# Order of the recurrence's exponential, spreading and state products, and attention positions computed four sequences ahead

## The chip, the cores and the metric

The kernel runs on one core of one Trainium2 chip. The metric is the device time of one execution in microseconds. The core's engines work side by side and meet at semaphores: TensorE (PE, and PEld for its weight loads), VectorE (DVE), ScalarE (ACT), GpSimd (POOL), and SyncE (SP), whose queue issues the transfers.

## The reference

The reference is an audio tower of four layers on 64 sequences of 250 frames (246 tokens after the front end), width 128. Two of its parts matter here; both are cut to their core.

The delta-rule attention of layer 2 walks over the batch axis as its time: 64 steps, for each of 246 positions (`bsz`) and 8 heads of size 64, once for `z` and then for the recurrence:

```python
def rec_step(carry, inp):
    R, h = carry
    zt, kt, vt, bt = inp
    qh = jax.nn.softmax(h, axis=-1)
    v_old = jnp.einsum('bhij,bhj->bhi', R, kt)
    R = R + (bt * (vt - v_old))[..., :, None] * kt[..., None, :]
    h = zt + jnp.einsum('bhij,bhj->bhi', R, qh)
    return ((R, h), h)
```

The kernel has the rows `u = bt * (vt - v_old)` from an earlier stage, so a step is h[t] = zz[t] + ri * sum over s up to t of (k[s] . e) u[s], with e the exponential of h[t-1] less its maximum, and ri one over the sum of e.

The relative attention of layer 3, for each of 64 sequences:

```python
matrix_bd = jnp.matmul(q_v, p.transpose(0, 1, 3, 2))
matrix_bd = rel_shift(matrix_bd)[:, :, :, :T] * scale
scores = jnp.matmul(q_u, k.transpose(0, 1, 3, 2)) * scale + matrix_bd
attn = jax.nn.softmax(scores, axis=-1)
out = jnp.matmul(attn, v)
```

## The kernel before

The kernel is a row of stages, each with its own buffers and semaphores; a stage consists of blocks, in which every engine has its own hand-written order, and at the end of a block all engines meet. Two stages are touched.

**Recurrence (`recur_stage`).** `run` is called 8 times, for pairs of heads and halves of the positions. One run holds 123 positions by 2 heads, split in group 0 (62 positions, 124 chains) and group 1 (61, 122 chains), one chain to a partition, and goes through SL = 64 steps t. In a step below HC = 32, each group `a` passes these operations:

- VectorE `dots(a, t)`: the product of the keys so far with `e` (L2945, 64 x n elements with n = t+1), its sum (L2950), and the weights `w` (L2954), which release TensorE;
- TensorE `turn(a, t)`: transposes `w` into `wT` (L2866);
- ScalarE `spread(a, t)`: writes `wT` into the block-diagonal `W` (L2816);
- TensorE `recent(a, t)`: the products of `W` with the values, into `acc` (L2894); one block of values up to 16 steps, two above;
- VectorE `finish(a, t)`: `acc` times the reciprocal plus `H` (L2964), and its maximum (L2965);
- ScalarE `exped(a, t)`: the exponential and its sum (L2828), on which the next `dots` of the group waits.

For 12 <= t < 32 (`inside`) VectorE puts `finish(1, t-1)` between the product and the sum of group 0. From step HC on, the 32 first steps act through a state: `make_state(n)` on TensorE (L2908) computes the state of 8 positions from keys and values (`Ks`, `Us`), `keep_state(n)` on ScalarE copies it (L2834). There are NR = 16 such parts, one in each step from RT0 = 14 to 29, of which TensorE does each between `recent(0, t)` and `turn(1, t)`, and ScalarE each after `spread(0, t)`. From step 32 on, `state(a, t)` multiplies with them, and ScalarE already has the exponential of group 0 ahead of group 1's spreading. The first state product of step 32 waits for `turn_exp`, which stands behind `recent(1, 31)`.

**Relative attention (`relative_stage`).** G = 16 sequences make one pass. For a new sequence j of a pass ("positions"): A projects queries, B multiplies them with the position matrix in 8 parts, ScalarE's `kept` copies these to `BD` (L3839, two buffers in turn; it waits until the store of two sequences before has landed), and SP stores them to `scr` in DRAM (L3622). The skewed read back from `scr` into `sc` (L3607, three buffers in turn) gives the shifted matrix. For a current sequence: projections (C, V; the values are written at L3767), scores S, softmax, T transposes, P, O. PSUM is a ring of four buffers through which all these products pass in the order that `order` lists.

`step_of(new, cur)` writes a pass: positions for the 16 sequences of block `new`, and everything else for the 16 of block `cur`. Before, a prologue makes positions for block 0 alone, three loop passes do block i with the positions of block i+1, and a last pass does block 3 without any. The read of current sequence j+2 is issued on SP when the scores of j-1 have been turned.

Of the kernel before, what the change touches and what calls it, by code (L numbers as in the profile page):

```python
# [12 lines left out]
B = 64  # L13
# [3 lines left out]
T = TIN - CTX + 1  # L17
# [2197 lines left out]
SL = B  # L2215
# [469 lines left out]
def recur_stage(nc, c, kr, ur, zz, hs):  # L2685


    SC, HC = 16, 32
# [6 lines left out]
    with Stage(nc, "recur") as st:  # L2695
# [72 lines left out]
        def run(i, half, following):  # L2768
            with st.step() as block:
# [40 lines left out]
                @block.scalar  # L2810
                def _(act):
                    def spread(a, t):
                        n = t % HC + 1
                        act.wait_ge(s_tr[a], t + 1)
                        r, b = (8 * n, 1) if n <= SC else (128, 2)
                        nc.scalar.activation(W[a][0:r, 0:b].rearrange("p b (g x) -> p b g x", x=40)[:, :, :, 0:8],  # L2816
                                             wT[a][0:r, 0:b].rearrange("p b (g x) -> p b g x", x=8), ACT.Copy).then_inc(s_dg[a], 1)

                    def spread_exp(a, t):
                        tg = GROUPS[a][1]  # L2820
                        act.wait_ge(s_et[a], t - HC + 1)
                        nc.scalar.activation(E[a][:, 0:34 * TG].rearrange("p (m x) -> p m x", x=34)[:, 0:tg, 0:2],
                                             eT[a][:, 0:2 * tg].rearrange("p (m h) -> p m h", h=2), ACT.Copy).then_inc(s_eg[a], 1)

                    def exped(a, t):
                        cp = 2 * GROUPS[a][1]
                        act.wait_ge(s_mx[a], t + 1)
                        nc.scalar.activation(e[a][0:cp], Hh[a][0:cp, t, :], ACT.Exp, bias=mx[a][0:cp, 0:1],  # L2828
                                             accum_out=rs[a][0:cp, 0:1]).then_inc(s_ex[a], 1)

                    def keep_state(n):
                        a, m0, nm = positions(n)
                        act.wait_ge(s_rm, n + 1)
                        nc.scalar.activation(R[a][:, m0:m0 + nm, :], Rp[n % 2][:, 0:nm, :], ACT.Copy).then_inc(s_rc, 1)  # L2834

                    for t in range(SL):
                        if t > HC:
                            exped(1, t - 1)
                            spread(0, t)
                            spread_exp(1, t)  # L2840
                        else:
                            if inside(t):
                                exped(1, t - 1)
                            spread(0, t)
                            if t and not inside(t):
                                exped(1, t - 1)
                            if t == HC:
                                spread_exp(1, t)
                        if RT0 <= t < RT0 + NR:
                            keep_state(t - RT0)  # L2850
                        if t + 1 < SL and t >= HC:
                            exped(0, t)
                        spread(1, t)
                        if t + 1 < SL and t < HC:
                            exped(0, t)
                        if HC <= t + 1 < SL:
                            spread_exp(0, t + 1)

                @block.tensor
                def _(pe):  # L2860
# [50 lines left out]
                    for t in range(SL):  # L2911
                        if t and t % SC == 0:
                            pe.wait_ge(s_in[t // SC], 16 * 24)
                        if t < HC:
                            for a in range(2):
                                turn(a, t)
                                recent(a, t)
                                if a == 0 and RT0 <= t < RT0 + NR:
                                    make_state(t - RT0)
                            if t == HC - 1:  # L2920
                                turn_exp(0, HC)
                        else:
# [563 lines left out]
def relative_stage(nc, c, xnT, pT, Wq, bq, Wk, bk, Wv, bv, Wo, bo, pu, pv_, scr, h, h_out):  # L3486


    SCALE = HD ** -0.5
    G = 16  # L3490
    NR = 3
    QH = NH // 2
    SCORES_AT = {0: 0, 2: 1, 5: 2, 7: 3}
    with Stage(nc, "rel") as st:
# [75 lines left out]
                dve.wait_ge(s_g, 1)  # L3570
                own(V.tensor_tensor(brow[:], brow[:], ring[0][0:HT, 0, 0:D], ALU.add))

        xblk = lambda n: xnT[:, bass.ds(n * (G * T), G * T)]
        rows = lambda t, n: t.rearrange("(i n p) d -> i p n d", n=2 * G, p=HT)[n]

        def step_of(new, cur):

            NX = new is not None
            CU = cur is not None
            proj = lambda j: [("A", j)] * NX + [("C", j), ("V", j)] * CU  # L3580
            order = proj(0)
            for j in range(G + 2):
                for q in range(8 if j < G else 0):
                    order += [("S", j, SCORES_AT[q])] if CU and q in SCORES_AT else []
                    order += [("B", j, q)] * NX
                    order += [("O", j - 2)] * (CU and j >= 2 and q == 3)
                if CU and j >= G:
                    order.append(("O", j - 2))
                if j + 1 < G:
                    order += proj(j + 1)  # L3590
                if CU and 1 <= j <= G:
                    order += [("T", j - 1, q) for q in range(4)] + [("P", j - 1)]
# [6 lines left out]
            with st.step() as block:  # L3599
                @block.sync  # L3600
                def _(sp):
# [4 lines left out]
                                n = p.stop - p.start  # L3606
                                sp.dma_start(sc[j % NR][p, f], bass.AP(scr.tensor, o, [[NH * WB - 1, n], [WB, NH], [1, T]])).then_inc(s_bd[j % NR][f], 16)  # L3607

                    if NX:
                        sp.dma_start(xa[:].rearrange("p a t -> p (a t)"), xblk(new)).then_inc(s_xa, 16)  # L3610
                    if CU:
                        sp.dma_start(xc[:].rearrange("p a t -> p (a t)"), xblk(cur)).then_inc(s_xc, 16)
                        for j in range(2):
                            positions(j)
                        for p in PARTS:
                            sp.dma_start(hb[p], rows(h, cur)[p]).then_inc(s_hb, 16)
                    for j in range(G + 2):
                        if NX and j < G:
                            for f in range(2):
                                sp.wait_ge(s_da, act_upto("B", j, 4 * f + 3))  # L3620
                                for p in PARTS:
                                    sp.dma_start(scr[new * (2 * G) + (2 * j + f)][p], BD[j % 2][f][p]).then_inc(s_bw[j % 2], 16)  # L3622
                        if CU and j + 2 < G:
                            if j:
                                sp.wait_ge(s_g, at["T", j - 1, 3] + 1)
                            positions(j + 2)
                        if CU and j >= 2:
                            sp.wait_ge(s_dd, dve_upto("O", j - 2))
                            for p in PARTS:
                                sp.dma_start(rows(h_out, cur)[p, 2 * j - 4:2 * j - 2], hb[p, 2 * j - 4:2 * j - 2]).then_inc(s_out, 16)  # L3630
                    if NX:
                        for k in range(2):
                            sp.wait_ge(s_bw[k], 64 * (G // 2))
                    if CU:
                        sp.wait_ge(s_out, 32 * G)

# [1 line left out]
                def _(pe):  # L3638
# [82 lines left out]
                        ins.then_inc(s_g, 1)  # L3721

                    def project(j):
                        if NX:
                            queries_next(j)
                        if CU:
                            queries_keys(j)
                            values(j)

                    project(0)  # L3730
                    for j in range(G + 2):
                        for q in range(8 if j < G else 0):
                            if CU and q in SCORES_AT:
                                scores(j, SCORES_AT[q])
                            if NX:
                                positions(j, q)
                            if CU and j >= 2 and q == 3:
                                outs(j - 2)
# [10 lines left out]
                def _(dve):  # L3749
# [5 lines left out]
                                                      hp[:].unsqueeze(2).to_broadcast(full), ALU.add, ALU.mult)  # L3755

                    def projected(j):
                        if NX:
                            dve.wait_ge(s_g, at["A", j] + 1)
                            masked(QV, slot("A", j), 3).then_inc(s_dd, 1)  # L3760
                        if CU:
# [59 lines left out]
                def _(act):  # L3821
# [25 lines left out]

                    for j in range(G + 1):
                        for q in range(8):
                            if NX and j < G:  # L3850
                                kept(j, q)
                            if CU and j and q < 4:
                                exped(j - 1, q)
# [1 line left out]
                            for q in range(4):  # L3855
                                turned(j - 1, q)

        step_of(0, None)
        with nc.Fori(0, B // G - 1) as i:
            step_of(i + 1, i)  # L3860
        step_of(None, B // G - 1)


def last_stage(nc, c, Wg, bg, We, be, h, out):
# [306 lines left out]
```

## Time and profile before

| | |
|---|---|
| median of 3 runs | 18497.64 us |
| lowest to highest | 18490.13 to 18520.3 us |
| profiled execution | 18509.24 us |
| its span, first to last instruction | 18507.2 us |
| mean granted TensorE clock | 0.787 of full speed |
| PE busy | 13100.1 us (71%) |
| DVE busy | 10585.8 us (57%) |
| ACT busy | 6518.6 us (35%) |
| recurrence, all 8 runs | about 10212 to 15040 us of the span |
| attention: prologue | first issue at 16300.77 us |
| attention: three loop passes | first issues at 16479.34, 16919.81 and 17359.78 us |
| attention: last pass | first issue at 17796.96 us, next stage at 18207.04 us |

Busy time counts an engine's instructions, not its waits. Times in rows are microseconds from the span's start. A line number is the kernel's, or that of the helper that records the operation: all projections and products of the attention stage show as L3640.

### The profile page before, as it was taken

What the parts mean: (1) busy time and instruction counts of PE and PEld (TensorE: products, weight loads), DVE (VectorE), ACT (ScalarE), POOL (GpSimd) and SP (SyncE); (2) the same over time, 40 slices, a digit from 0 to 9 for tenths busy, and PEclk for the clock granted to TensorE, in tenths of its full rate; (3) what the DMA queues carried; (4) which work ended last, traced back from release to release, by engine and by line L of the source; (5) the groups of instructions that cost most, each with busy time, mean ns of one, the idle gap of its engine ahead of it and who ended that gap; (6) DMA issues with size and microseconds to landing.
All of it is one profiled execution on the core that took longest, in us unless ns stands there. A gap on an engine that the chain in (4) does not pass through costs nothing. (4 is left out here: it accounts for less than half of the span.)

```text
span 18507.2 us, 593329 instructions
## 1 busy us (share of the span) xinstructions
PE 13100.1 (71%) x262069; PEld 10249.8 (55%) x262069; DVE 10585.8 (57%) x24424; ACT 6518.6 (35%) x16019; POOL 2265.2 (12%) x1394
## 2 busy tenths in 40 slices
PE   4607778862847888888888667766677675867777
PEld 3505666651535676766766455555555564735555
DVE  6451457763144555555555676767776745346664
ACT  3101246640214565665665112121211121345541
POOL 0048100003541111111111000000000000000001
PEclk9556578875868999999999667866787697967775
DMA  0313320121331111111111222021211153177752
GB/s 22 106 30 46 69 48 21 33 77 45 65 76 46 24 26 26 26 24 26 26 24 26 47 42 43 19 44 38 45 33 28 38 129 93 39 228 195 195 136 68
DMA packets 1835030, 1095.27 MB, mean 59 GB/s; under 512 B 1109166, under 2 KB 1763409, under 8 KB 1814481
## 3 DMA queue, kind: packets, MB, share of 16 engines
q1 hardware_dynamic: 1605063, 999.32, 22.4%
q0 software_dynamic: 227328, 57.19, 2.1%
q8 instruction: 2092, 34.28, 0.8%
q14 instruction: 547, 4.48, 0.1%
HBM read 569.43 MB, written 484.53 MB: 57 GB/s over the span
## 5 line engine op out<-in xcount | busy, mean ns | idle before, releaser
L2894 PE MATMUL recur_acc<-recur_U,recur_W 8*32 8x64 f32 (+4 forms) x49152 | 1402.4, 270 | 510.3 <-ACT recur_W L2816 428.5
L2894 PEld LDWEIGHTS recur_acc<-recur_U,recur_W 8*32 8x32 f32 (+4 forms) x49152 | 1068.8, 140 | 928.8 <-ACT recur_W L2816 738.6
L2945 DVE TENSOR_TENSOR recur_pr<-recur_K,recur_e 124x64 f32<-124x64 f32 (+60 forms) x1024 | 1282.0, 1252 | 395.9 <-ACT recur_e L2828 395.6
L2881 PE MATMUL recur_acc<-recur_R,recur_E 128*32 128x64 f32 x62976 | 1206.6, 232 | 247.1 <-issue 235.4
L2950 DVE TENSOR_REDUCE recur_dot<-recur_pr 124x1 f32<-124x64 f32 (+60 forms) x1024 | 1281.8, 1252 | 29.8
L2881 PEld LDWEIGHTS recur_acc<-recur_R,recur_E 128*32 128x32 f32 x62976 | 1070.1, 118 | 350.0 <-issue 294.0
L2475 ACT ACTIVATE delta_B0l<-delta_pS 64x256 f32<-64x256 f32 x1968 | 743.4, 378 | 875.4 <-PE delta_pS L2375 857.9
L2816 ACT ACTIVATE recur_W<-recur_wT 128x256 f32<-128x256 f32 (+16 forms) x1024 | 335.1, 327 | 1961.2 <-PE recur_wT L2866 1960.0
L2866 PE MATMUL recur_wT<-const_ident,recur_w 128*128 128x128 f32 (+15 forms) x1536 | 479.5, 375 | 768.1 <-DVE recur_w L2954 760.9
L2475 ACT ACTIVATE delta_B1l<-delta_pS 64x256 f32<-64x256 f32 x1968 | 743.6, 378 | 698.8 <-PE delta_pS L2375 678.2
L2375 PE MATMUL delta_pM<-delta_B1l 64*64 64x128 f32 (+1 forms) x11808 | 737.2, 255 | 140.8 <-ACT delta_B1l L2478 140.3
L2375 PE MATMUL delta_pM<-delta_B0l 64*64 64x128 f32 (+1 forms) x11808 | 720.8, 256 | 66.5 <-ACT delta_B0l L2478 66.4
L2510 POOL TENSOR_TENSOR delta_QK<-delta_QK,delta_mx 128x512 f32<-128x512 f32 x369 | 384.6, 1042 | 3116.3 <-DVE delta_mx L2563 3116.3
L2375 PE MATMUL delta_gp<-delta_W,delta_xc 128*128 128x512 f32 x1230 | 696.0, 650 | 54.8 <-DVE delta_xc L2546 36.1
L2375 PEld LDWEIGHTS delta_pM<-delta_B1l 64*64 64x64 f32 x11808 | 602.6, 134 | 165.0 <-ACT delta_B1l L2478 158.7
L2375 PE MATMUL delta_gp<-delta_KT 64*64 64x64 f32 x11808 | 563.5, 224 | 183.7 <-ACT delta_KT L2497 143.2
L2375 PEld LDWEIGHTS delta_pM<-delta_B0l 64*64 64x64 f32 x11808 | 580.8, 133 | 197.1 <-issue 112.9
L2866 PEld LDWEIGHTS recur_wT<-const_ident,recur_w 128*128 128x128 f32 (+15 forms) x1536 | 168.9, 143 | 931.4 <-DVE recur_w L2954 833.9
L2964 DVE SCALAR_TENSOR_TENSOR recur_H<-recur_acc,recur_ri,recur_H 124x64 f32<-124x64 f32 (+1 forms) x1024 | 284.8, 278 | 676.2 <-PE recur_acc L2894 669.1
L2828 ACT ACTIVATE recur_e<-recur_H,recur_mx 124x64 f32<-124x64 f32 x1008 | 346.8, 344 | 915.6 <-DVE recur_mx L2965 915.3
L2375 PE MATMUL delta_pM<-delta_B 64*64 64x128 f32 x7872 | 548.1, 278 | 136.1 <-issue 87.5
L3188 POOL IOTA choice_ios<- 123x64 f32 x1 | 0.2, 184 | 5245.6 <-POOLq L78 5245.6
(620 smaller groups left out, 34022.7 us busy)
## 6 DMA issues: line engine op xcount, KB each, us to landing
scr<-rel_BD SPq DMA_DIRECT2D x128, 1288.0 KB
rel_sc<-scr SPq DMA_DIRECT2D x128, 861.0 KB
xnT<-ln_xT SPq DMA_DIRECT2D x64, 492.0 KB, 3.0
kr<-delta_QK SPq DMA_DIRECT2D x492, 64.0 KB, 2.4
ur<-delta_Uf SPq DMA_DIRECT2D x492, 64.0 KB, 2.3
zz<-delta_Z SPq DMA_DIRECT2D x492, 64.0 KB, 2.2
recur_K<-kr SPq DMA_DIRECT2D x64, 448.0 KB
recur_H<-zz SPq DMA_DIRECT2D x64, 448.0 KB
```

The lines of the kernel that those rows point to most:

```text
L2375: return nc.tensor.matmul(o, l, r, start=True, stop=True)
L2475: ins = nc.scalar.activation(new[h, :, 0, :], pS[k][HALF[1 - x], 0:4, :], ACT.Copy)
L2510: nc.gpsimd.tensor_tensor(third(j), third(j), mx[:, rows_of(j)].unsqueeze(2).to_broadcast([128, FH, FD]), ALU.subtract).then_inc(s_sh, 1)
L2816: nc.scalar.activation(W[a][0:r, 0:b].rearrange("p b (g x) -> p b g x", x=40)[:, :, :, 0:8], wT[a][0:r, 0:b].rearrange("p b (g x) -> p b g ...
L2828: nc.scalar.activation(e[a][0:cp], Hh[a][0:cp, t, :], ACT.Exp, bias=mx[a][0:cp, 0:1], accum_out=rs[a][0:cp, 0:1]).then_inc(s_ex[a], 1)
L2866: ins = nc.tensor.transpose(wT[a][0:8 * k, b, :], w[a][:, SC * b:SC * b + k, :].rearrange("p s k -> p (s k)"), c.ident[:])
L2881: nc.tensor.matmul(acc[a][32 * q:32 * q + 32, 0:FD], E[a][:, EQ * q + 32 * j:EQ * q + 32 * j + 32], R[a][:, m, :], start=(j == 0), stop=False)
L2894: ins = nc.tensor.matmul(acc[a][32 * q:32 * q + 32, 0:FD], W[a][0:8 * k, b, 160 * q + 32 * j:160 * q + 32 * j + 32], U[a][0:8 * k, 2 * (t ...
L2945: V.tensor_tensor(pr[0:cp, 0:n, :], K[a][0:cp, r0:r0 + n, :], e[a][0:cp, None, :].to_broadcast([cp, n, FD]), ALU.mult).then_inc(s_own[a], 1)
L2950: own[a](V.tensor_reduce(dot[a][0:cp, 0:n], pr[0:cp, 0:n, :], AX.X, ALU.add))
L2964: own[a](V.scalar_tensor_tensor(Hh[a][0:cp, t, :], acc[a][0:cp, 0:FD], ri[a][0:cp, 0:1], Hh[a][0:cp, t, :], ALU.mult, ALU.add))
L3188: nc.gpsimd.iota(ios[:], pattern=[[1, CS]], base=0, channel_multiplier=0, allow_small_or_imprecise_dtypes=True).then_inc(s_po, 1)
```

## The change

In the recurrence, steps 12 to 31: ScalarE takes `exped(0, t)` before `spread(1, t)` in place of after it, as it does from step 32 on. TensorE makes the state part of a step after `recent(1, t)` in place of before `turn(1, t)`. ScalarE keeps it one step later, before `spread(0, t)`.

In the attention stage, `step_of` takes the first new sequence, the current block and the number of sequences ahead. The prologue makes positions of LAG = 4 sequences; loop pass i those of sequences 16i+4 to 16i+19; the last pass those of the last 12. So a stored position matrix can be read in the pass that writes it, and SP gets a wait for its store ahead of the read.

```diff
                             if inside(t):
                                 exped(1, t - 1)
+                            if RT0 < t <= RT0 + NR:
+                                keep_state(t - 1 - RT0)
                             spread(0, t)
...
-                        if RT0 <= t < RT0 + NR:
-                            keep_state(t - RT0)
-                        if t + 1 < SL and t >= HC:
+                        early = t >= HC or inside(t)
+                        if t + 1 < SL and early:
                             exped(0, t)
                         spread(1, t)
-                        if t + 1 < SL and t < HC:
+                        if t + 1 < SL and not early:
                             exped(0, t)
...
                             for a in range(2):
                                 turn(a, t)
                                 recent(a, t)
-                                if a == 0 and RT0 <= t < RT0 + NR:
-                                    make_state(t - RT0)
+                            if RT0 <= t < RT0 + NR:
+                                make_state(t - RT0)
...
+    LAG = 4
...
-        xblk = lambda n: xnT[:, bass.ds(n * (G * T), G * T)]
+        xblk = lambda first, count: xnT[:, bass.ds(first * T, count * T)]
...
-        def step_of(new, cur):
-
-            NX = new is not None
+        def step_of(new, cur, ahead):
+
+            NX = lambda j: j < ahead
...
-                        sp.dma_start(xa[:].rearrange("p a t -> p (a t)"), xblk(new)).then_inc(s_xa, 16)
+                        sp.dma_start(xa[:, 0:ahead, :].rearrange("p a t -> p (a t)"), xblk(new, ahead)).then_inc(s_xa, 16)
...
                         if CU and j + 2 < G:
                             if j:
                                 sp.wait_ge(s_g, at["T", j - 1, 3] + 1)
+                            n = j + 2 - LAG
+                            if n >= 0:
+                                sp.wait_ge(s_bw[n % 2], 64 * (n // 2 + 1))
                             positions(j + 2)
...
-        step_of(0, None)
+        step_of(0, None, LAG)
         with nc.Fori(0, B // G - 1) as i:
-            step_of(i + 1, i)
-        step_of(None, B // G - 1)
+            step_of(i * G + LAG, i, G)
+        step_of(B - G + LAG, B // G - 1, G - LAG)
```

The remaining lines replace the condition `NX` by `NX(j)`, and the block counts by sequence counts.

## Rows read from the trace of the kernel before

**Rows 1.** Windows, steps 12 to 31, then after step 32: busy, count; clock, DMA
```profile
10275.00:10480.00 205.00, 126.11 (x2836) 96.16 (x2835) 162.79 (x240) 38.67 (x137) 0.00 (x0) 0.50 0.08 17
...
10483.00:10513.00 30.00, 24.73 (x1052) 19.98 (x1054) 9.55 (x44) 6.29 (x26) 0.00 (x0) 0.90 0.10 22
```
**Rows 2.** Grouped lines, whole span, then 10275 to 10480: busy, mean ns, idle before
```profile
L2945 DVE TENSOR_TENSOR recur_pr<-recur_K,recur_e 124x64 f32<-124x64 f32 (+60 forms) x1024 | 1282.0, 1252 | 395.9 <-ACT recur_e L2828 395.6
...
L2945 DVE TENSOR_TENSOR recur_pr<-recur_K,recur_e 124x832 f32<-124x832 f32 (+39 forms) x40 | 65.9, 1649 | 35.8 <-ACT recur_e L2828 35.8
```
**Rows 3.** Timeline, steps 21 to 22: start, duration, engine, operation, [idle before, releaser]
```profile
10364.50 1.97 PE L2908 MATMUL recur_Rp<-recur_Us,recur_Ks 32*64 32x64 f32 x32
10364.55 0.34 DVE L2954 TENSOR_TENSOR recur_w<-recur_dot,recur_par 122x176 f32<-122x176 f32 x1
...
10365.18 0.22 DVE L2965 TENSOR_REDUCE recur_mx<-recur_H 124x1 f32<-124x64 f32 x1
...
10366.40 0.69 PE L2866 MATMUL recur_wT<-const_ident,recur_w 128*128 128x128 f32 x2
...
10367.12 0.38 ACT L2816 ACTIVATE recur_W<-recur_wT 128x256 f32<-128x256 f32 x1
...
10367.40 0.34 ACT L2828 ACTIVATE recur_e<-recur_H,recur_mx 124x64 f32<-124x64 f32 x1
...
10367.56 2.09 PE L2894 MATMUL recur_acc<-recur_U,recur_W 128*32 128x64 f32 x64 [0.47 <-ACT recur_W L2816]
10367.64 0.19 ACT L2828 ACTIVATION_READ_ACCUMULATOR recur_e<-recur_H,recur_mx 124x1 f32 x1
...
10367.86 1.69 DVE L2945 TENSOR_TENSOR recur_pr<-recur_K,recur_e 124x1472 f32<-124x1472 f32 x1 [2.46 <-ACT recur_e L2828]
...
10369.72 0.28 DVE L2964 SCALAR_TENSOR_TENSOR recur_H<-recur_acc,recur_ri,recur_H 122x64 f32<-122x64 f32 x1 [0.16 <-PE recur_acc L2894]
...
10371.88 0.35 DVE L2954 TENSOR_TENSOR recur_w<-recur_dot,recur_par 124x184 f32<-124x184 f32 x1
```
**Rows 4.** Timeline of the attention's prologue: its load, first product, fourth and sixteenth copies
```profile
16300.77 0.33 SPq L3610 DMA_DIRECT2D rel_xa<-xnT  x1
...
16307.83 1.19 PE L3640 MATMUL rel_ring<-rel_xa,rel_w 128*128 128x246 f32 x2 [9.42 <-DMA rel_xa<-xnT]
...
16337.58 5.52 ACT L3839 ACTIVATE rel_BD<-rel_ring 123x736 f32<-123x736 f32 x8 [5.08 <-DMA scr<-rel_BD]
...
16459.46 5.52 ACT L3839 ACTIVATE rel_BD<-rel_ring 123x736 f32<-123x736 f32 x8 [3.79 <-DMA scr<-rel_BD]
```
**Rows 5.** Timeline, loop pass, then last pass: first issue, first and thirteenth values
```profile
16479.34 0.38 SPq L3610 DMA_DIRECT2D rel_xa<-xnT  x1
...
16494.55 0.68 DVE L3767 TENSOR_TENSOR rel_Vp<-rel_ring,rel_mk 123x512 f32<-123x512 f32 x1
...
16786.81 0.68 DVE L3767 TENSOR_TENSOR rel_Vp<-rel_ring,rel_mk 123x512 f32<-123x512 f32 x1
...
17796.96 0.37 SPq L3612 DMA_DIRECT2D rel_xc<-xnT  x1
...
17807.23 0.68 DVE L3767 TENSOR_TENSOR rel_Vp<-rel_ring,rel_mk 123x512 f32<-123x512 f32 x1
...
18086.69 0.68 DVE L3767 TENSOR_TENSOR rel_Vp<-rel_ring,rel_mk 123x512 f32<-123x512 f32 x1
```
**Rows 6.** Timeline: one-block products; VectorE's product at steps 17 and 31
```profile
10295.67 1.08 PE L2894 MATMUL recur_acc<-recur_U,recur_W 120*32 120x64 f32 x32 [0.47 <-ACT recur_W L2816]
...
10314.15 1.36 DVE L2945 TENSOR_TENSOR recur_pr<-recur_K,recur_e 124x1152 f32<-124x1152 f32 x1 [2.69 <-ACT recur_e L2828]
...
10468.43 2.29 DVE L2945 TENSOR_TENSOR recur_pr<-recur_K,recur_e 124x2048 f32<-124x2048 f32 x1 [0.97 <-ACT recur_e L2828]
```
**Rows 7.** Timeline of a loop pass: reads of a sequence's positions, that sequence's values
```profile
16611.76 2.12 SPq L3607 DMA_DIRECT2D rel_sc<-scr  x4
...
16633.48 0.68 DVE L3767 TENSOR_TENSOR rel_Vp<-rel_ring,rel_mk 123x512 f32<-123x512 f32 x1
```

More of the change, by code:

```diff
@@ L3571, in _ @@
                 own(V.tensor_tensor(brow[:], brow[:], ring[0][0:HT, 0, 0:D], ALU.add))
-        xblk = lambda n: xnT[:, bass.ds(n * (G * T), G * T)]
+        xblk = lambda first, count: xnT[:, bass.ds(first * T, count * T)]
         rows = lambda t, n: t.rearrange("(i n p) d -> i p n d", n=2 * G, p=HT)[n]
-        def step_of(new, cur):
-            NX = new is not None
+        def step_of(new, cur, ahead):
+            NX = lambda j: j < ahead
             CU = cur is not None
-            proj = lambda j: [("A", j)] * NX + [("C", j), ("V", j)] * CU
+            proj = lambda j: [("A", j)] * NX(j) + [("C", j), ("V", j)] * CU
             order = proj(0)
@@ L3584, in step_of @@
                     order += [("S", j, SCORES_AT[q])] if CU and q in SCORES_AT else []
-                    order += [("B", j, q)] * NX
+                    order += [("B", j, q)] * NX(j)
                     order += [("O", j - 2)] * (CU and j >= 2 and q == 3)
@@ L3607, in positions @@
                                 sp.dma_start(sc[j % NR][p, f], bass.AP(scr.tensor, o, [[NH * WB - 1, n], [WB, NH], [1, T]])).then_inc(s_bd[j % NR][f], 16)
-                    if NX:
-                        sp.dma_start(xa[:].rearrange("p a t -> p (a t)"), xblk(new)).then_inc(s_xa, 16)
+                    if ahead:
+                        sp.dma_start(xa[:, 0:ahead, :].rearrange("p a t -> p (a t)"), xblk(new, ahead)).then_inc(s_xa, 16)
                     if CU:
-                        sp.dma_start(xc[:].rearrange("p a t -> p (a t)"), xblk(cur)).then_inc(s_xc, 16)
+                        sp.dma_start(xc[:].rearrange("p a t -> p (a t)"), xblk(cur * G, G)).then_inc(s_xc, 16)
                         for j in range(2):
@@ L3617, in _ @@
                     for j in range(G + 2):
-                        if NX and j < G:
+                        if NX(j):
                             for f in range(2):
@@ L3621, in _ @@
                                 for p in PARTS:
-                                    sp.dma_start(scr[new * (2 * G) + (2 * j + f)][p], BD[j % 2][f][p]).then_inc(s_bw[j % 2], 16)
+                                    sp.dma_start(scr[new * 2 + (2 * j + f)][p], BD[j % 2][f][p]).then_inc(s_bw[j % 2], 16)
                         if CU and j + 2 < G:
@@ L3630, in _ @@
                                 sp.dma_start(rows(h_out, cur)[p, 2 * j - 4:2 * j - 2], hb[p, 2 * j - 4:2 * j - 2]).then_inc(s_out, 16)
-                    if NX:
+                    if ahead:
                         for k in range(2):
-                            sp.wait_ge(s_bw[k], 64 * (G // 2))
+                            sp.wait_ge(s_bw[k], 64 * (ahead // 2))
                     if CU:
@@ L3723, in project @@
                     def project(j):
-                        if NX:
+                        if NX(j):
                             queries_next(j)
@@ L3734, in _ @@
                                 scores(j, SCORES_AT[q])
-                            if NX:
+                            if NX(j):
                                 positions(j, q)
@@ L3757, in projected @@
                     def projected(j):
-                        if NX:
+                        if NX(j):
                             dve.wait_ge(s_g, at["A", j] + 1)
@@ L3849, in _ @@
                         for q in range(8):
-                            if NX and j < G:
+                            if NX(j):
                                 kept(j, q)
```

## The prediction

> **What bounds the kernel now.** I read first the page of the profile: no engine is full, so the kernel is a row of stages with limits of their own, and only two of them are touched. For the first, the recurrence, I read the granted clock and the grouped lines of a stretch that covers steps 12 to 31 of one run, then the timeline of one step there. For the second, the relative-position attention, I read its timeline at the prologue, at a loop pass and at the last pass.
>
> In steps 12 to 31 of a run, 205 us, VectorE is the engine that everything turns around, and it sits idle 35.8 us in 20 waits for group 0's exponential; the whole span has 395.6 us of that wait, 49.5 for each of the 8 runs, so 35.8 of a run's 49.5 lie here [rows 2]. The timeline of step 21 shows why [rows 3]. Group 1's weights `w` are ready to be turned at 10364.55+0.34 = 10364.89; call this point A. VectorE finishes group 0 and has its maximum at 10365.18+0.22 = A+0.51. The exponential could start then. But TensorE makes state products until 10366.4, only then turns group 1's weights, ScalarE spreads them at 10367.12, and the exponential, queued behind that spreading, starts at 10367.40. VectorE goes on at 10367.86, 2.46 us after its maximum.
>
> In the attention stage, the prologue computes positions for 16 sequences alone. ScalarE needs 5.52 us for each, but waits for the store of two sequences before: its start moves from 16337.58 to 16459.46 in 12 sequences, 10.16 us each, released by the DMA [rows 4]. From its first values to its thirteenth a loop pass takes 24.4 us a sequence, the last pass, which has no positions, 23.3 [rows 5].
>
> **Part 1, the recurrence (steps 12 to 31 of 8 runs).** After the edit the exponential of group 0 follows the maximum at once. Row by row: maximum at A+0.51, exponential 0.04 later (A+0.55; an estimate, ScalarE takes a turn 0.03 after its end at 10367.09), VectorE goes on 0.46 after its start, as 10367.40 to 10367.86 does: A+1.01. So each wait becomes 0.50 us. What is late next is group 1: its spreading now stands behind the exponential and its accumulator read. These end at +0.43 (0.24 from exponential to read, 0.19 the read), A+0.98; from spreading to products is 0.44 (10367.12 to 10367.56), and from products to the finish that waits for them 2.16 (10367.56 to 10369.72): A+3.58 [rows 3]. VectorE is ready for that finish 0.08 before its product of length D ends: A+0.93+D. So a new wait of 2.65-D stands in front of "finish group 1". D is 1.36 us at step 17 and 2.29 at step 31, 0.066 more with each step [rows 6]; the 15 waits sum to 15 x 2.65 less 15 x 1.825, or 12.4 us. Steps 13 to 16 follow one block: the products take 1.08 in place of 2.09 [rows 6] and I put the spreading 0.1 shorter, so the wait is about 1.54-D, with D from 1.10 to 1.29 by the same slope: 1.4 us for the four.
>
> The same formula gives what this wait is today: the products start at 10367.56, 0.30 before VectorE's own product, so it is 1.94-D, or 2.8 us over steps 17 to 25 (at step 22 it is 0.25; the row's 0.16 is counted from the product's nominal end). Sum for one run: before 35.8+2.8 = 38.6; after 0.67 for step 12 (it has the old order ahead of it; 0.67 is what steps 12 to 14 show), 19 x 0.50 = 9.5, 12.4 and 1.4, or 24.0. Gain 14.6. At step 32 the state products queue behind group 1's recent products, which are 0.43 later against A, so 14.2 remain. Times 8: **114 us**. Steps 13 to 16 are where the edit's two sides nearly cancel; steps 17 to 22 gain 1.3 to 1.6 us each.
>
> The state products move behind group 1's. TensorE is free of them at A+0.98+0.44+2.02+1.90 = A+5.34, and next has to turn group 0's weights, which follow the finish by 2.16+0.3 at step 22 (10369.72 to 10371.88, and its own time) and by 0.33 less at step 17: A+3.58+2.13 = A+5.7, and later with every step. So they are covered by VectorE's reduction, with 0.35 us to spare; if the cover were gone, each of 16 steps would lose up to the 1.97 us [rows 3]. Keeping the state moves a step on, to a time when ScalarE waits for the turned weights: 0.60 us, covered. The loads of state rows that SP issues after a state product have four steps before use.
>
> The price I can't see is how soon ScalarE takes a spreading behind an accumulator read. Least: 0.1 less (it starts a spreading 0.1 to 0.2 before the operation before it ends). Most: 0.43+0.1. That is 19 x 0.1 x 8 = 15 us either way. I take the end of the read, since the queue shows nothing nearer.
>
> **Part 2, positions four ahead.** Prologue: 12 sequences less at 10.16 = 121.9 us; the last stores' tail stays. Its load is a quarter as large: 7.1 us from issue to the first product today [rows 4]; the bounds of the new one are 7.1 (nothing saved) and 1.8 (in proportion); I take 3 saved. The last pass takes these 12 sequences. A loop pass goes from the first values to the thirteenth in 16786.81-16494.55 = 292.3 us, the last pass in 279.5 [rows 5]; the two other loop passes lie within 1.6 us of the first, so 12 us are added. From SP's first issue to the first values a loop pass takes 15.2 us, the last pass 10.3; the load ahead is three quarters of a pass's, so I add 3.5 of the 4.9. Net 121.9+3-12-3.5 = **109 us**. Bounds: 97 if the mix costs twice as much, 115 if the load shrinks in proportion and the start adds nothing.
>
> The added wait on SP (the store of sequence j-2 before the read of j+2) stands behind the wait for the turned scores and behind the stores of sequence j. ScalarE writes those of j only after the store of j-2 has landed, since the buffer is the same one. So it is always satisfied while new positions are made; the last two follow a sequence or more later. Cost nothing. Behind it stand the output's stores, which nobody waits for before the end.
>
> **Sum.** Profiled execution 18509.2 us (span 18507.2 and 2 around it): 18509.2-114-109 = 18286. The median of the three runs is 18497.6, 11.6 under it: **18274 us**, 1.2% less. About 0.2% (37 us) is what a measurement tells from no change.
>
> **Rivals.**
> *TensorE's clock rises in the changed steps.* It is 0.50 there now, the 1.2 GHz level, and 0.90 right after step 32, where the engine is busy 24.7 of 30 us [rows 1]. In step 21 it works two turns, two sets of recent products and the state products, about 7.5 of 11.0 us; after the change 7.5 of 9.7, 77%, which comes near. Against it: its longest unbroken stretch, 7 us in step 21, gets looser, not denser. At 2.4 GHz the products take about half, the new waits go, and up to 12.4 x 8 = 99 us come on top; for half the steps 50: about 18175 to 18225. Chance 0.10. The Trainium skill (TensorE: Matmul & The Clock Gate, Part 1, "What's actually happening") says that the throttled state is the default and that activity releases it; by that rule this rival would hold, while the trace shows 0.50 kept over the dense stretch of every step.
>
> *Only one half works.* If the state products are not covered, or group 1's lateness costs what the exponential gains, Part 1 gives nothing: 18389. If the mixed last pass ran at the sum of both (23.3 us, and 5.5 of ScalarE's copying), Part 2 would give 12 x 4.5 = 54 less: 18328. Together 0.14, most of it between 18300 and 18390.
>
> *Slower: the reads wait for landed stores.* If the new wait on SP really held, each of 54 reads would come late. A read is issued at 16611.76, behind the turned scores, and its first sum follows the values at 16633.48, 22 us later [rows 7]; the transfer takes no more than the 10.16 us of a larger store. So 12 us of lateness are free, and from 12+4.1 us on (223 us over 54 reads) the gain is gone; at 17 us of lateness the reads cost 5 x 54 = 270, which gives 18544. The stores are issued two sequences, 50 us, before. Chance 0.02.
> The Trainium skill (DMA: Bandwidth & Descriptors, "Two DMAs through the same engine are not ordered") demands such a wait on the first transfer's completion wherever a second reads its bytes; before, the end of each pass gave it, and no run here shows its price in the middle of a pass.
>
> **How the numbers follow.** Forecast as summed, 18240 to 18305: 0.72. Clock: 0.10. One half: 0.14. Slower or nothing: 0.04. The range 18205 to 18330 holds the first, a third of the clock's and half of the third. Faster by over 0.2%: 0.96; within: 0.02; slower: 0.02.
>
> **What the profile after would show.** Right: VectorE's wait for the exponential about 0.50 us in every step from 13 to 31 (sum 10, not 35.8), a wait for group 1's products of 1.3 us at step 17 falling to 0.36 at step 31, 190 us for the stretch at clock 0.50; the prologue 54 us long, the last pass 426; SP without a wait for stores. Wrong: a clock over 0.5 in the stretch; TensorE turning group 0's weights late, behind the state products; VectorE waiting for positions read back.

## The result, and the profile after

The changed kernel takes 18265.32 us (median of 4 runs, 18245.1 to 18276.77), the kernel before 18496.94 (18490.13 to 18520.3): a ratio of 0.987, interval 0.9856 to 0.9883, or 231.6 us less. The forecast was 223 us less. The profiled execution took 18245.1 us, the fastest of its four, with a span of 18242.8 us, 264.4 under that of before.

I cut both spans at the same instructions. Lengths are differences of starts in the timeline; a step starts where VectorE starts group 0's product:

| Stage | before | after | change |
|---|---|---|---|
| recurrence, group 0's first to its last product, over the 8 runs | 4813.3 | 4666.7 | -146.6 |
| of it, steps 12 to 31 (start of step 12 to start of step 32), each run | 205.5 | 187.2 | -18.3 (x8 = -146) |
| of it, steps 32 to 62 (start of step 32 to start of step 63), sum of 8 | 2506.9 | 2509.1 | +2.2 |
| attention, prologue | 178.6 | 52.4 | -126.2 |
| attention, three loop passes | 1317.6 | 1318.4 | +0.8 |
| attention, last pass | 410.1 | 427.1 | +17.0 |
| stages ahead of the recurrence (not touched) | 10212.8 | 10204.1 | -8.7 |

The two stages give 255.0 of the 264.4 us; 8.7 are a stage that the change leaves alone.

The grouped lines of the page and of steps 12 to 31 (busy, mean ns, idle before and its releaser) answer to [rows 2]. The last of them is of the kernel before, in its own window from 10275 to 10480: the finishes, which [rows 2] don't have.

```profile
L2946 DVE TENSOR_TENSOR recur_pr<-recur_K,recur_e 124x64 f32<-124x64 f32 (+60 forms) x1024 | 1281.8, 1252 | 192.4 <-ACT recur_e L2828 192.2
...
L2946 DVE TENSOR_TENSOR recur_pr<-recur_K,recur_e 124x832 f32<-124x832 f32 (+39 forms) x40 | 65.9, 1648 | 10.4 <-ACT recur_e L2828 10.4
...
L2965 DVE SCALAR_TENSOR_TENSOR recur_H<-recur_acc,recur_ri,recur_H 122x64 f32<-122x64 f32 (+1 forms) x40 | 11.1, 277 | 9.6 <-PE recur_acc L2895 9.2
...
L2964 DVE SCALAR_TENSOR_TENSOR recur_H<-recur_acc,recur_ri,recur_H 122x64 f32<-122x64 f32 (+1 forms) x40 | 11.0, 275 | 2.9 <-PE recur_acc L2894 2.6
```

The wait for the exponential fell from 35.8 to 10.4 us, and a wait for group 1's products has taken part of its place: 9.6 us in front of the finishes, where before had 2.9. In both kernels 0.8 us of that stand in front of group 0's finishes, so group 1's part is 8.8 after and 2.1 before. VectorE's own work did not move (65.9 us for the 40 products in both), so the stretch is shorter by idle time. The windows of the whole stretch and of the attention's prologue and last pass, of the kernel after (start and end, length, busy time and count of PE, PEld, DVE, ACT and POOL, granted clock, DMA share, GB/s):

```profile
10266.45:10454.00 187.55, 127.03 (x2848) 96.33 (x2841) 164.22 (x243) 39.09 (x136) 0.00 (x0) 0.50 0.08 18
...
16145.00:16197.00 52.00, 24.92 (x136) 12.27 (x136) 2.92 (x4) 22.07 (x32) 0.00 (x0) 0.63 0.69 233
17515.00:17943.00 428.00, 330.31 (x2648) 242.36 (x2648) 270.78 (x300) 208.25 (x320) 8.83 (x1) 0.76 0.64 172
```

The clock of the stretch is 0.50 as it was: the rival in which it rises did not come about. The timeline of steps 21 to 22 after the change is the one to hold against [rows 3]:

```profile
10345.85 0.34 DVE L2955 TENSOR_TENSOR recur_w<-recur_dot,recur_par 122x176 f32<-122x176 f32 x1
...
10346.25 0.69 PE L2867 MATMUL recur_wT<-const_ident,recur_w 128*128 128x128 f32 x2 [0.38 <-DVE recur_w L2955]
10346.48 0.22 DVE L2966 TENSOR_REDUCE recur_mx<-recur_H 124x1 f32<-124x64 f32 x1
10346.74 0.35 ACT L2828 ACTIVATE recur_e<-recur_H,recur_mx 124x64 f32<-124x64 f32 x1 [3.01 <-DVE recur_mx L2966]
10346.99 0.18 ACT L2828 ACTIVATION_READ_ACCUMULATOR recur_e<-recur_H,recur_mx 124x1 f32 x1
10347.08 0.36 ACT L2816 ACTIVATE recur_W<-recur_wT 128x256 f32<-128x256 f32 x1
10347.21 1.69 DVE L2946 TENSOR_TENSOR recur_pr<-recur_K,recur_e 124x1472 f32<-124x1472 f32 x1 [0.51 <-ACT recur_e L2828]
...
10347.50 2.09 PE L2895 MATMUL recur_acc<-recur_U,recur_W 128*32 128x64 f32 x64 [0.56 <-ACT recur_W L2816]
...
10349.52 1.97 PE L2909 MATMUL recur_Rp<-recur_Us,recur_Ks 32*64 32x64 f32 x32
10349.66 0.28 DVE L2965 SCALAR_TENSOR_TENSOR recur_H<-recur_acc,recur_ri,recur_H 122x64 f32<-122x64 f32 x1 [0.76 <-PE recur_acc L2895]
...
10351.53 0.60 ACT L2834 ACTIVATE recur_R<-recur_Rp 128x512 f32<-128x512 f32 x1 [0.86 <-PE recur_Rp L2909]
...
10351.82 0.35 DVE L2955 TENSOR_TENSOR recur_w<-recur_dot,recur_par 124x184 f32<-124x184 f32 x1
...
10352.23 0.69 PE L2867 MATMUL recur_wT<-const_ident,recur_w 128*128 128x128 f32 x2 [0.74 <-DVE recur_w L2955]
```

The exponential follows the maximum by 0.04 us (10346.70 to 10346.74) and VectorE is held 0.51 us. Group 1's weights are turned at once, since no state products stand in front of them. The finish of group 1 now waits 0.76 us for its products. The state products end at 10351.49, and TensorE is then idle 0.74 us before group 0's weights: the cover that the forecast counted on is there. (A cover is work of VectorE long enough to hide TensorE's.)

The attention's timeline after: the prologue's first issue, its second and last pair of values kept, the next pass's issue, then first issue, first and thirteenth values and end of the last pass. It answers to [rows 4, 5]:

```profile
16145.19 0.33 SPq L3612 DMA_DIRECT2D rel_xa<-xnT  x1
...
16168.04 5.52 ACT L3844 ACTIVATE rel_BD<-rel_ring 123x736 f32<-123x736 f32 x8 [4.23 <-DMA scr<-rel_BD]
16177.45 5.52 ACT L3844 ACTIVATE rel_BD<-rel_ring 123x736 f32<-123x736 f32 x8 [3.90 <-PE rel_ring L3645]
...
16197.55 0.38 SPq L3612 DMA_DIRECT2D rel_xa<-xnT  x1
...
17515.91 0.37 SPq L3612 DMA_DIRECT2D rel_xa<-xnT  x1
...
17529.76 0.68 DVE L3772 TENSOR_TENSOR rel_Vp<-rel_ring,rel_mk 123x512 f32<-123x512 f32 x1
...
17822.90 0.68 DVE L3772 TENSOR_TENSOR rel_Vp<-rel_ring,rel_mk 123x512 f32<-123x512 f32 x1
...
17943.02 0.88 SPq L3924 DMA_DIRECT2D last_H<-hA  x2
```

And the waits of SP's queue in that last pass (waited for, us in total, times, longest):

```profile
SPq L3624 <- ACT rel_BD L3844: 143.4, 20, 9.5
SPq L3609 <- PE rel_ring L3703: 105.0, 13, 20.6
SPq L3635 <- DVE rel_hb L3803: 58.9, 4, 23.2
SPq L3640 <- DMA hA<-rel_hb: 1.2, 1, 1.2
```

No wait here ends with a landed store of positions: the line of the added wait, L3630, is missing, and it is missing over all four passes too. From first to thirteenth values the last pass takes 293.1 us, as a loop pass does.

### The profile page after: what moved, and what is told of

It is laid out like the page before. It is cut to its first block and busy times, and to the rows that moved or that the text cites. A ratio compares the mean times of both kernels' runs of the same rounds, so it can differ in the third digit from the quotient of the medians.

```text
span 18242.8 us, 593377 instructions
## 1 busy us (share of the span) xinstructions
PE 13067.4 (72%) x262069; PEld 10226.4 (56%) x262069; DVE 10594.1 (58%) x24424; ACT 6519.8 (36%) x16019; POOL 2265.4 (12%) x1394
## 5 line engine op out<-in xcount | busy, mean ns | idle before, releaser
L2375 PE MATMUL delta_gp<-delta_W,delta_xc 128*128 128x512 f32 x1230 | 695.6, 649 | 54.7 <-DVE delta_xc L2546 35.8
L1207 POOL DMA_INDIRECT hB<-experts_y,experts_idx x256 | 619.1, 2418 | 102.0 <-issue 80.6
```

What stands on the lines that cost most here:

```text
L1207: nc.gpsimd.indirect_dma_start(acc[:, :], bass.IndirectOffsetOnAxis(ap=idx[:, e, 4 * q + t:4 * q + t + 1], axis=0), y[n % 3][:, t, :], Non ...
L2375: return nc.tensor.matmul(o, l, r, start=True, stop=True)
```

## The experiments

Each kernel is the changed one with the edit shown. They ran on other chips, where the kernel before takes 18558 to 18567 us, so each is compared with the kernel before, and mostly also with the changed one, on its own chip. What differs there is above all steps 32 to 62 (2530 to 2560 us in sum, 2507 and 2509 on the first chip) and the stages ahead of the recurrence (10213 to 10251 us, 10213 and 10204 on the first chip), while steps 12 to 31 of one order of work agree to 0.1 us on every chip. So small differences are read from the length of the stage, not from the median.

### First set: each part alone (the kernel before there 18557.87)

**The exponential moved, the state products left between the groups.**

```diff
                             turn(a, t)
                             recent(a, t)
-                            if RT0 <= t < RT0 + NR:
-                                make_state(t - RT0)
+                                if a == 0 and RT0 <= t < RT0 + NR:
+                                    make_state(t - RT0)
```
(and the state kept between the two spreadings, behind the exponential)

> The changed kernel, but in steps 14 to 29 TensorE makes the state products between group 0's recent products and group 1's turn, as in the kernel before, and ScalarE keeps them in the same step, behind the exponential. So only the exponential moves. Theory A (what must go is the state products' time in front of group 1's turn; the exponential alone only moves the wait): VectorE's wait for the exponential falls to about 0.5 us, but group 1's products still come at A+4.83, so the wait for them is about 3.9-D, 2.2 us at step 22 where it was 0.25. The sum of both stays, and the recurrence gains 0 to 20 us in all 8 runs; the kernel comes out 109 to 130 us under the one before, about 18380. Theory B (the exponential behind group 1's spreading is what costs): most of the recurrence's gain stays, the kernel is near 18265 to 18300.

Measured: 18441.69 us, ratio 0.9937 (0.992 to 0.9953), 116 less than before; steps 12 to 31 take 203.5 us. The grouped lines of this kernel for that stretch, and rows of its timeline in step 22:

```profile
L2946 DVE TENSOR_TENSOR recur_pr<-recur_K,recur_e 124x832 f32<-124x832 f32 (+39 forms) x40 | 65.9, 1649 | 10.4 <-ACT recur_e L2828 10.4
...
L2965 DVE SCALAR_TENSOR_TENSOR recur_H<-recur_acc,recur_ri,recur_H 122x64 f32<-122x64 f32 (+1 forms) x40 | 11.1, 277 | 25.8 <-PE recur_acc L2895 25.7
```

```profile
10364.22 1.97 PE L2909 MATMUL recur_Rp<-recur_Us,recur_Ks 32*64 32x64 f32 x32
10366.12 0.69 PE L2867 MATMUL recur_wT<-const_ident,recur_w 128*128 128x128 f32 x2
...
10369.43 0.28 DVE L2965 SCALAR_TENSOR_TENSOR recur_H<-recur_acc,recur_ri,recur_H 122x64 f32<-122x64 f32 x1 [2.12 <-PE recur_acc L2895]
```

The wait for the exponential is the same 10.4 us as with both moves, and yet only 2.0 us of the 205.5 are gone: 25.8 us stand in front of the finish in its place. The state products still delay the turning of group 1's weights, and VectorE meets that delay 2 us later. This edit alone does little more than move the wait.

**The state products moved, the exponential left behind group 1's spreading.**

```diff
-                        early = t >= HC or inside(t)
+                        early = t >= HC
```

> The changed kernel, but in steps 12 to 31 the exponential of group 0 stands behind group 1's spreading again, as in the kernel before. So only the state products and their keeping move. Theory A: the wait for the exponential is about 1.0 us in steps 17 to 31 and that for group 1's products as before, 1.94-D; 15.0+2.8+3.4 = 21.2 us a run where it was 38.6, so the recurrence gains 17 us a run, as much as with both moves, and the kernel comes out within 15 us of the changed one. Theory B: the recurrence gains less than half, the kernel is at 18320 or above.

Measured: 18312.18 us, 0.9866 (0.985 to 0.9883), 246 less; steps 12 to 31 take 187.6 us, 0.4 more than with both moves. ScalarE's keeping of the state moves here too, with the products; no run separates those two.

```profile
L2946 DVE TENSOR_TENSOR recur_pr<-recur_K,recur_e 124x832 f32<-124x832 f32 (+39 forms) x40 | 65.9, 1649 | 17.9 <-ACT recur_e L2828 17.9
...
L2965 DVE SCALAR_TENSOR_TENSOR recur_H<-recur_acc,recur_ri,recur_H 122x64 f32<-122x64 f32 (+1 forms) x40 | 11.0, 275 | 2.8 <-PE recur_acc L2895 2.6
```

Idle 17.9+2.8 = 20.7 us, against 10.4+9.6 = 20.0 with both. Whichever of the two small operations of ScalarE goes first, the other is late by about as much. Of the recurrence's 18.3 us a run, 17.9 come with the state products' move. The other 0.4 is the exponential that step 32 waits for: step 31 takes 12.23 us here and 11.82 with both moves.

**The positions alone.** The function of the recurrence as before the change, that of the attention as after it.

> The recurrence of the kernel before, the attention stage of the changed one. If the two halves add up, this gains 109 us (18388), the rest of the changed kernel's gain, 120 to 145, being the recurrence's. Rival: part of it is something between the stages, such as a start of later stages at another phase of TensorE's clock; then the halves do not add up within 20 us.

Measured: 18453.7 us, 0.9943 (0.9926 to 0.996), 104 less; attention 1800.9 us, steps 12 to 31 back at 205.5.

**The changed kernel again**, for the chip.

> The changed kernel once more, as the reference of this set: 18245 to 18280 us.

Measured: 18317.95 us, 0.9867 (0.9851 to 0.9884), 240 less. The halves add up within 10 us: 104 for the positions by the median, and 8 x 18.3 = 146 for the recurrence by the length of its stage.

### Second set: the terms by themselves (the kernel before there 18566.56)

**Positions two sequences ahead in place of four.** Now the store of a sequence's positions is the one just issued when the read of them comes up.

```diff
-    LAG = 4
+    LAG = 2
```

> The changed kernel with positions made two sequences ahead in place of four. Now the read of sequence j+2 waits on SP for the store of sequence j of the same pass step, which has only just been issued. Theory A (a read may come 12 us late for nothing): the wait on SP shows as a few us for each read, VectorE waits for none of them, the prologue is 19 us shorter, the last pass 2 us longer: 15 to 19 us faster than the changed kernel. Theory B (the landed store is on the path): VectorE waits for positions read back in every sequence, and 62 reads at 1 us and more make it slower than the changed kernel by 45 us and more.

Measured: 18320.62 us, 0.9866 (0.9849 to 0.9882), 246 less: by the median no gain over four ahead (240 less in the first set; the changed kernel did not run in this one), where 15 to 19 were expected. The attention took 1786.7 us, 12 to 24 less than the 1798.9 to 1810.8 of the runs with four ahead. SP's waits in the last pass of this kernel:

```profile
SPq L3630 <- DMA scr<-rel_BD: 83.9, 13, 13.7
```

Here the added wait does hold, 6.5 us a time and at most 13.7, and no wait of VectorE in the pass ends with a transfer: the reads are issued late and still land in time. The rival "the reads wait for landed stores" counted 12 us of lateness as free; two ahead is the case that comes near it, and it is free still.

**Every state product made twice**, into the same place, to see what cover it has behind group 1.

```diff
-                            for m in range(nm):
+                            for m in [*range(nm), *range(nm)]:
```

> The changed kernel, but every state product is done twice (the second writes the same result over the first), so 1.97 us more of TensorE in each of steps 14 to 29. Theory A (the state products are covered by VectorE's product and sum, with 0.35 us to spare at step 17 and 1.2 at step 29, and group 0's own products have slack behind): the loss falls from 1.7 us at step 17 to nothing at step 25 or so, 8 to 10 us a run, 65 to 90 us in all. Theory B (they stand in the chain as they did in the kernel before): 16 x 1.97 x 8 = 252 us.

Measured: 18397.73 us, 0.9902 (0.9886 to 0.9919), 77 more than e4's kernel and 77 to 80 more than the changed one as measured in the other sets; steps 12 to 31 take 195.4 us, 8.2 more, x8 = 66. The window over the stretch of this kernel and two finishes of group 0 in it:

```profile
10313.00:10508.00 195.00, 151.71 (x3328) 122.34 (x3322) 164.23 (x240) 38.59 (x135) 0.00 (x0) 0.50 0.08 18
```

```profile
10348.82 0.28 DVE L2965 SCALAR_TENSOR_TENSOR recur_H<-recur_acc,recur_ri,recur_H 124x64 f32<-124x64 f32 x1 [1.73 <-PE recur_acc L2895]
...
10420.77 0.28 DVE L2965 SCALAR_TENSOR_TENSOR recur_H<-recur_acc,recur_ri,recur_H 124x64 f32<-124x64 f32 x1 [0.21 <-PE recur_acc L2895]
```

The doubled products take 3.68 us of a step's timeline where the single ones take 1.97, 1.71 more, and they stick out of their cover: VectorE waits for group 0's products 1.73 us in step 16, 0.21 in step 23 (the rows above), and not at all from step 24 on. In step 17 it waits 1.52 us, where the changed kernel has 0.24: of the 1.71 us more, 0.43 were covered. So the single products had that much to spare there, and more in later steps, as VectorE's pieces grow.

**The finish of group 1 behind group 0's sum in steps 17 to 31, in place of between product and sum**, so that the 0.76 us of the timeline above would be filled.

```diff
-                        dots(0, t, before if inside(t) else None, before if both else None)
+                        dots(0, t, before if 12 <= t < 17 else None, before if both or 17 <= t < HC else None)
```

> The changed kernel, but in steps 17 to 31 VectorE finishes group 1's last step behind group 0's sum in place of between its product and its sum. Theory A (the wait that took the old one's place, up to 1.2 us before that finish, is only there because VectorE asks for group 1's products too early): it goes, and a wait of 0.25 us for group 1's exponential comes in; 6 us a run, 40 to 55 us in all, about 18215. Theory B (TensorE or ScalarE would then be the limit): the wait moves to group 0's products, and nothing is gained.

Measured: 18301.18 us, 0.9853 (0.9837 to 0.987), 265 less than before; steps 12 to 31 take 184.0 us, 3.3 less, x8 = 26, where I had expected 6 a run and 40 to 55 in all. Grouped lines of this kernel, and a step of its timeline:

```profile
L2946 DVE TENSOR_TENSOR recur_pr<-recur_K,recur_e 124x832 f32<-124x832 f32 (+39 forms) x40 | 66.3, 1656 | 12.8 <-ACT recur_e L2828 12.1
...
L2965 DVE SCALAR_TENSOR_TENSOR recur_H<-recur_acc,recur_ri,recur_H 122x64 f32<-122x64 f32 (+1 forms) x40 | 11.1, 276 | 2.3 <-PE recur_acc L2895 1.7
```

```profile
10337.53 0.28 DVE L2965 SCALAR_TENSOR_TENSOR recur_H<-recur_acc,recur_ri,recur_H 122x64 f32<-122x64 f32 x1
...
10338.57 1.43 DVE L2946 TENSOR_TENSOR recur_pr<-recur_K,recur_e 122x1216 f32<-122x1216 f32 x1 [0.21 <-ACT recur_e L2828]
...
10342.14 0.28 DVE L2965 SCALAR_TENSOR_TENSOR recur_H<-recur_acc,recur_ri,recur_H 124x64 f32<-124x64 f32 x1 [0.26 <-PE recur_acc L2895]
```

The wait for products goes from 9.6 to 2.3 us, as intended, but 2.4 come back in front of the product (0.21 in this step: group 1's exponential is now late). That leaves 4.9 us less idle time for 3.3 us less length. The other 1.6 us are busy time: from the start of step 12 to that of step 32 VectorE is busy 165.5 us here, 163.9 in the changed kernel. Why the reordered pieces take that much more is not shown.

### Third set, five rounds: the small differences (the kernel before there 18562.79)

> The changed kernel again, the reference of this set: about 240 us under the kernel before on the same chip.

> Positions two ahead once more, beside the changed kernel on one chip. In the profile of e4_lag2 the attention stage was 1786.7 us long against 1798.9 to 1810.8 in the kernels of the same day with four ahead, while its median showed no gain. If the stage is what counts and the rest is scatter of other stages, it is 10 to 20 us faster than the changed kernel; if the shorter stage is paid back elsewhere, 0.

> Group 1's finish behind group 0's sum in steps 17 to 31, once more. The profile shows 171.9 us for steps 12 to 31 where the changed kernel has 175.4: 8 runs give 28 us.

> The late finish and positions two ahead together. The two stages have nothing in common, so 28 and 17 add up to 45 us under the changed kernel, a quarter of a per cent; 30 to 55.

| Kernel | median, us | ratio to before | attention, us |
|---|---|---|---|
| changed kernel | 18321.15 | 0.9864 (0.9848 to 0.988) | 1800.4 |
| positions two ahead | 18293.37 | 0.9859 (0.9843 to 0.9875) | 1787.3 |
| late finish | 18300.52 | 0.9858 (0.9842 to 0.9874) | 1799.9 |
| both of these | 18282.59 | 0.984 (0.9826 to 0.9854) | 1790.7 |

The added wait holds again with two ahead, here over all four passes:

```profile
SPq L3630 <- DMA scr<-rel_BD: 333.1, 52, 14.7
```

Four more waits for such a store, one a pass and 36.0 us in all, stand under the line of the reads (L3609).

The intervals overlap, so the medians alone don't separate these kernels. The stage lengths do for the parts: 10 to 13 us in the attention, 3.3 x 8 = 26 in the recurrence. By the medians two ahead is 28 us under the changed kernel, more than its stage explains and than the 10 to 20 expected, and the late finish 21, where 28 were expected. The kernel with both has the lowest median, 39 us under the changed kernel (45 expected, 30 to 55) and 1.5% under the one before.

## Why the prediction was right

Point by point, by its own steps.

**Exponential after the maximum at once: right.** Predicted 0.04 us behind the maximum and a wait of 0.50; the timeline has 0.04 and 0.51, and the sum is 10.4 us where 0.67+9.5 = 10.2 was predicted.

**What is late next is group 1: right in kind, too large.** Predicted was a wait of 12.4+1.4 = 13.8 us; group 1's part of the 9.6 is 8.8. The wait at step 17 is 1.09 us (1.3 predicted), at step 31 nothing (0.36). Four causes stand in the timeline:

- The finish of group 1 follows the start of group 0's product by 2.45 us (10347.21 to 10349.66), where the forecast has A+3.58 less A+1.01, 2.57. Of the 0.12 us, 0.09 are ScalarE's: it takes group 1's spreading 0.34 us behind the exponential's start (10346.74 to 10347.08), before the accumulator read ends, not 0.43. That is the price that the prediction called unseen and bounded at 0.1 a step. Over 15 steps the 0.12 make 1.8 us.
- From step 25 on the products take 1.93 us, not 2.09, as the row of step 28 below shows: 7 x 0.16 = 1.1 us.
- Steps 13 to 16 come 0.6 us under their part of the forecast.
- The remaining 1.5 us are a matter of counting. The forecast counts a wait from 0.08 us before the product's nominal end, where VectorE would take an unhindered finish, and the profile from that end: 19 x 0.08.

```profile
10408.77 1.93 PE L2895 MATMUL recur_acc<-recur_U,recur_W 128*32 128x64 f32 x64 [0.56 <-ACT recur_W L2816]
...
10410.78 0.28 DVE L2965 SCALAR_TENSOR_TENSOR recur_H<-recur_acc,recur_ri,recur_H 122x64 f32<-122x64 f32 x1 [0.20 <-PE recur_acc L2895]
```

**The term of the sum that was mis-sized is Part 1: 14.2 us a run predicted; measured 18.3 over steps 12 to 31, 146 us in all 8 runs in place of 114.** The prediction's 190 us for the stretch are 187.2. Its price for group 1's lateness, 13.8 less 2.8 or 11.0 us, was 7.5: the first three causes above, 3.5 us. Another 0.4 is a wait that it did not count, the one of step 32 for group 0's exponential: step 31 takes 11.82 us, where it took 12.24. The later start of the state products at step 32, for which it set 0.43 us aside, fits what the runs show: step 32 is 0.31 us longer in the mean of 8 runs, and steps 32 to 62 together 0.27. The idle time of the two groups fell by 18.7 us, from 35.8+2.9 to 10.4+9.6, and that of step 32's first operation by 0.5; 0.9 us of this do not show in the length, for a finish that waits no longer overlaps the end of the product (VectorE is busy 163.9 us of the stretch, 163.0 before).

**A remark beside the sum was wrong.** The prediction says that in steps 13 to 16 the edit's two sides nearly cancel. Those four steps are 4.2 us shorter, almost a quarter of the gain: before, the exponential's wait was already 1.90, 1.83 and 2.69 us at the starts of steps 15, 16 and 17. The sum has these waits in its 35.8 us, so the remark changed nothing in it. For steps 17 to 22 it gave 1.3 to 1.6 us each; they gained 1.2 to 1.6.

**State products covered: right, and with the margin that was said.** Predicted were 0.35 us to spare at step 17 and 0.33 more at step 22; TensorE is idle 0.36 us at step 17 between the state products and group 0's weights, and 0.74 at step 22. With the products doubled, e5 loses 8.2 us a run, so the cover is real and short.

**To which edit the gain belongs** the prediction did not say; it priced both as one. It is the state products' move. e2 has 17.9 of the 18.3 us; e1 has 2.0 us a run, 16 us in all; with the first made, the second adds 0.4 us a run.

**Prologue: 52.4 us, predicted 54.** 126.2 us less against 121.9+3. **Loop passes:** unchanged, within 0.8 us in sum. **Last pass:** 427.1, predicted 426: +17.0 against +15.5. The first values come 13.85 us after the first issue ([rows 5]: 10.3 before; +3.6 for the 3.5 assumed) and twelve sequences take 293.1 us, the price of a mixed pass. Net 108.4 for the predicted 109, and e3 shows it alone, 104.

**Wait for landed stores: free, as argued.** It does not appear in SP's waits. The rival's price was worked out for 54 reads; the code puts the wait ahead of 12 reads a pass, 48 in all, so 17 us of lateness would have cost 240 us and not 270, which doesn't change which case happened. It was not for lack of a real transfer to wait for: with two ahead it holds up to 14.7 us, and even then the attention gets shorter, because the prologue loses another two sequences (57.0 to 33.7 us in the third set).

**The rivals.** The clock did not rise. Neither half failed. The case that was left, both parts near their sums, is what happened: 18265 for 18274. Part of that closeness is luck: in the profiled run Part 1 gave some 32 us more than forecast and untouched stages gave 9 more, while the median of after lies 20 us above the profiled run, where I had set it 12 below.

## What to carry to other kernels

When a small operation waits behind another in one queue, look at what holds the first one up before reordering the two: here swapping the exponential and the spreading gained 2.0 us a run alone and 0.4 beside the other move, and taking 2 us of ready but unurgent matmuls from in front of both gained 17.9. Ask of every wait that an edit removes where the same lateness arrives next, and price that place with the lengths of the pieces around it, since it shrinks or vanishes as they grow. Work that can run at any time within a step belongs behind the last operation that someone waits for, as long as it ends before the next one; doubling it on the chip tells how much room there is.

## What the runs showed that was not expected

- ScalarE started the next activation 0.09 us after the start of the accumulator read, ahead of that read's nominal end (10346.99, 0.18 long; 10347.08). The pair costs the follower 0.34 us, not the sum of 0.43.
- TensorE's clock stayed at 0.50, the 1.2 GHz level, in steps 12 to 31 even with the state products doubled, when it was busy 151.7 of 195 us, 78%. The window below, of the kernel before, has 0.92 with 244.75 of 325.5 us, 75%; it starts in step 34 of the first run and takes in 12 us of the second. Cut at 10800, the end of the first run, it has 0.95 with 231.5 of 297.5 us, 78% again. What makes the difference, no run here shows.

```profile
10502.50:10828.00 325.50, 244.75 (x10609) 193.04 (x10601) 224.40 (x452) 65.75 (x251) 0.00 (x0) 0.92 0.13 27
```

- Steps 12 to 31, at clock 0.50, repeat to 0.1 us on the first and three other chips. Steps 32 to 62 differ by up to 53 us in sum, and not only between chips: on one chip the kernels of the second set lie 28 us apart, those of the third 25. How much of that is the edits and how much scatter is not separated.
- Waiting for a landed store and then reading it back cost 6.4 us a time on SP (333.1 us in 52 waits) with two sequences of distance, and nothing at all with four.
